# Counting edges for 16 nodes at a time instead of 32, with eight source parts instead of four

## The chip, the cores and the metric

The kernel runs on one core of one Trainium2 chip. The metric is the device time of one execution in microseconds (us); where several runs are given, their median counts. Lower is better.

## What is computed

One layer of a graph network on 1250 nodes with 768 features and 41250 edges (20000 random pairs in both directions and a loop for each node, sorted by target). Cut to what matters:

```
xn  = layernorm(x)
x   = x + gat(gat1(xn), edges) + random_feature_attention(xn) @ proj
x   = x + mixture_of_experts(layernorm(x))

gat:  e = leaky_relu(al_s[src] + al_d[dst]);  softmax of e over the edges of a target
      out = segment_sum(h[src] * alpha, dst)
mix:  phi = exp(x_head @ rf - |x_head|^2 / 2)
      out = phi_q @ (phi_k^T v) / (phi_q @ sum(phi_k))
```

The kernel does not walk the edges in the two attention layers. It first counts, for each target node and each source node, how many edges run between them, and then works with the dense 1250 x 1250 table of counts.

## The kernel before

The program goes through phases one after the other: a norm phase (`norm_phase`), two halves of the random feature attention (`mix_half_phase`, four heads each, followed by `numerator`), the projection, the two graph layers, and the experts. Each phase is a block with one instruction stream per engine; semaphores order the streams within it, and the block ends when all engines are through.

The table of counts is made in the mix halves, among the matrix products. `norm_phase` loads the edges, 128 to a row and 324 rows (`EROWS`), and turns them so that a row of edges lies along the 128 partitions. For each edge it makes a key, target times `SPLIT` plus the part of the source (`keyT`), and the source's place in its part of `SLO` nodes (`sloT`). A window is a group of `WIN` target nodes, so `WIN * SPLIT` is 128 keys, and there are `NW` windows. For each window `norm_phase` also works out which rows of edges can hold its targets (`spans`, lines 280 to 313): the start of the second step and the end, in steps of `RB` rows, two steps at least. An all-reduce over partitions on GpSimd stands in the middle of that.

In a mix half, VectorE makes for each row of edges two tables of zeros and ones, `CA` (128 edges by 128 keys, line 665, one operation for all rows of a step) and `CB` (128 edges by `SLO` places, line 671, one operation a row). TensorE multiplies them (line 807), and the sum over the rows of a window in one PSUM tile `S` is the table of counts for these targets, 128 by `SLO`. A short product (line 818) closes the sum, ScalarE copies it out of PSUM (line 729), and SyncE stores it in DRAM (line 636). The tables lie in a ring of `RING` steps. VectorE and TensorE both load the two numbers of a window's span into registers (lines 620 and 621), run the first step, and then loop over the others; a step's place in the ring is worked out in registers too, and so are the addresses of its rows. With `RB` 5, 40 windows and two steps each there are 400 rows.

The half itself goes over ten tiles of 125 nodes. For tile t TensorE turns q and k (`turn`, line 773), makes the q, k and v products of the next tile (`gemm`, line 762, twelve matmul records each), the features of k (`features`, line 781, in two parts of two heads) and keys times values (`keys_values`, line 790). The order is written out by hand, and so is the place of the two windows of a tile in it:

```
turn(0, t); gemm(0, t+1); window(2t); turn(1, t); gemm(1, t+1); features(t, 0)
window(2t+1); features(t, 1); gemm(2, t+1); keys_values(t)
```

The last tile of a half has no products of a next tile. ScalarE squares q and k for their norms (line 736), copies the turned q and k (lines 738 and 743), takes the exponential of the features (lines 747 and 750) and copies the counts, in a fixed order. VectorE evacuates q, k and v with their bias (lines 701 and 713), sums the squares (lines 706 and 707), makes the tables for the windows, and multiplies slices of the first graph weight with attention vectors (line 689).

Of the kernel before, what the change touches and what calls it, by code (L numbers as in the profile page):

```python
# [10 lines left out]
ALU = mybir.AluOpType  # L11
# [3 lines left out]
N = 1250  # L15
NT = 10
# [12 lines left out]
RB = 5  # L29
# [3 lines left out]
WIN = 32  # L33
NW = 40
SPLIT = 4
SLO = 314
# [102 lines left out]
def norm_phase(nc, cx, x, ident, xnT, src, dst, keyT, sloT, spans, counting, rf_dram, rfT, rf_loaded, load_next):  # L139
# [19 lines left out]
    DIV = (1 << DIV_SHIFT) // RB + 1  # L159
    assert FULL < EGP and EGP * EG == EROWS  # L160
    assert all(n * DIV >> DIV_SHIFT == n // RB for n in range(EROWS + RB))
    with ExitStack() as st:
# [63 lines left out]
        def _(dve):  # L226
# [4 lines left out]
            step(dve.tensor_scalar(hi[:], sf[:], float(SLO), None, ALU.is_ge))  # L231
            for part in range(2, SPLIT):
                step(dve.scalar_tensor_tensor(hi[:], sf[:], float(part * SLO), hi[:], ALU.is_ge, ALU.add))
# [339 lines left out]
def mix_half_phase(nc, cx, half, rfT, rf_loaded, xnT, ident, w, brow, w_loaded, b_loaded, attn, gnn_w1, a_src, a_dst,  # L573
# [6 lines left out]
    RING = 4  # L580
# [14 lines left out]
    with ExitStack() as st:  # L595
        qT = sb(nc, st, tag + "qT", [A, HH, N])
        kv = sb(nc, st, tag + "kv", [128, HH, 2, A])
        with ExitStack() as st1:
# [47 lines left out]
            def _(dve):  # L646
# [7 lines left out]
                with dve.register(tag + "count_turn_dve") as turn:  # L654
# [41 lines left out]
                    for t in range(NT):  # L696
# [12 lines left out]
                        window(PER * t)  # L709
                        dve.wait_ge(v_done, t + 1)  # L710
                        if t >= 1:
                            dve.wait_ge(kv_step, t)
# [3 lines left out]
                        window(PER * t + 1)  # L716
                        for n in range(t * columns // NT, (t + 1) * columns // NT):
                            attention_column(n)
                dve.wait_ge(kv_step, NT)
# [3 lines left out]
            @block.scalar  # L723
            def _(act):
                def keep_counts(i):
                    act.wait_ge(counted, i + 1)
                    if i >= 2:
                        act.wait_ge(s_stored[i % 2], 16 * (i // 2))
                    act.activation(cout[i % 2][:], S[:], ACT.Copy).then_inc(s_evac, 1)

                for t in range(NT):
                    for c, (evac, squared, ready) in enumerate(((q_evac, qsq, q_ready), (k_evac, ksq, k_ready))):
                        act.wait_ge(evac, t + 1)
                        if t >= 1:
                            act.wait_ge(ready, t)
                        act.activation(sq[:, c, :, :], qs[:, c, :, 0:MD], ACT.Square).then_inc(squared, 1)
                    act.wait_ge(q_turned, t + 1)
                    act.activation(qT[:, :, t * P:(t + 1) * P], TQ[:], ACT.Copy).then_inc(qT_done, 1)
                    keep_counts(PER * t)
                    act.wait_ge(k_turned, t + 1)  # L740
                    if t >= 1:
                        act.wait_ge(phi, 2 * t)
                    act.activation(kT[:], TQ[:], ACT.Copy).then_inc(kT_done, 1)
                    act.wait_ge(phi, 2 * t + 1)
                    if t >= 1:
                        act.wait_ge(kv_step, t)
                    act.activation(phik[:, 0:2, :], PH[:], ACT.Exp).then_inc(exped, 1)
                    keep_counts(PER * t + 1)
                    act.wait_ge(phi, 2 * t + 2)
                    act.activation(phik[:, 2:4, :], PH[:], ACT.Exp).then_inc(exped, 1)  # L750

            @block.tensor
            def _(pe):
# [31 lines left out]
                def keys_values(t, stop):  # L785
                    pe.wait_ge(exped, 2 * t + 2)
                    pe.wait_ge(v_evac, t + 1)
                    for h in range(HH):
                        for m in range(2):
                            last = pe.matmul(KV[h // 2][:, h % 2, m, :], phik[:, h, m * 128:(m + 1) * 128],  # L790
# [7 lines left out]
                with pe.register(tag + "count_turn_pe") as count:  # L798
# [25 lines left out]
                    for t in range(NT):  # L824
# [4 lines left out]
                        window(PER * t, *span(pe, half * PER * NT + PER * t))  # L829
                        turn(1, t)  # L830
                        if more:
                            gemm(1, t + 1, k_done, k_evac)
                        features(t, 0)
                        window(PER * t + 1, *span(pe, half * PER * NT + PER * t + 1))
                        features(t, 1)
                        if more:
                            gemm(2, t + 1, v_done, v_evac)
                        keys_values(t, not more)
# [1854 lines left out]
```

## Time and profile before

| | |
|---|---|
| median of 3 runs | 2090.27 us |
| lowest and highest | 2078.87 and 2092.76 us |
| the profiled execution's own time | 2086.34 us |
| its span, first to last instruction | 2084.6 us |
| mean granted TensorE clock | 0.977 |
| TensorE busy | 1991.5 us, 96% of the span |
| VectorE busy | 1168.3 us, 56% |
| ScalarE busy | 449.5 us, 22% |

The times of rows are microseconds from the start of the span. PE is TensorE's matmul, PEld its weight load, DVE VectorE, ACT ScalarE, POOL GpSimd, SP SyncE; a q behind an engine's name is its instruction queue with the register work, waits and branches, which doesn't count as busy. L807 is line 807 of the kernel. A matmul's end is modelled and reaches into the next one's time, so a block of matmuls lasts from its start to the next block's start.

### The profile page before, as it was taken

How to read it: one execution, taken by the hardware profiler on the slowest of the kernel's cores; microseconds unless marked ns; L12 is line 12 of the kernel's file. 1: busy time of each engine (PE TensorE's matmuls, PEld its weight loads, DVE VectorE, ACT ScalarE, POOL GpSimd, SP SyncE). 2: the span in 40 equal slices, each digit the busy share in tenths (PEclk: the TensorE clock that was granted, in tenths of full speed). 3: DMA queues.
4: the chain of work that ended last, by engine and by line, in shares of the span. 5: the costliest groups of instructions: out<-in, count | busy, mean ns of one | idle time of the engine just before them, and what ended most of it. 6: DMA issues, size and time to landing. Idle time of an engine off the chain costs nothing. (4 is left out here: it accounts for less than half of the span.)

```text
span 2084.6 us, 32353 instructions
## 1 busy us (share of the span) xinstructions
PE 1991.5 (96%) x9933; PEld 1469.9 (71%) x9934; DVE 1168.3 (56%) x2548; ACT 449.5 (22%) x822; POOL 176.6 (8%) x181
## 2 busy tenths in 40 slices
PE   4999899998989998999999999999997999999998
PEld 3666666666648887888888855556655777777776
DVE  6666436652565664888888652167764333333343
ACT  3222222222002321222222200004321222222222
POOL 0000000000000000000000000000001333222232
PEclk9999999998999999999999999999997999999999
DMA  7000220002645350743333244444225888899654
GB/s 257 22 17 20 93 107 17 20 17 74 217 120 171 121 155 32 221 146 102 122 101 112 82 153 156 151 134 142 90 74 196 271 249 241 252 284 289 180 136 83
DMA packets 81192, 282.79 MB, mean 136 GB/s; under 512 B 11689, under 2 KB 32225, under 8 KB 71490
## 3 DMA queue, kind: packets, MB, share of 16 engines
q1 hardware_dynamic: 59138, 211.02, 30.4%
q0 software_dynamic: 14848, 56.18, 11.1%
q10 hardware_dynamic: 7104, 14.26, 2.0%
q8 instruction: 59, 0.97, 0.2%
q14 instruction: 43, 0.35, 0.1%
HBM read 217.43 MB, written 63.99 MB: 135 GB/s over the span
## 5 line engine op out<-in xcount | busy, mean ns | idle before, releaser
L1379 PE MATMUL gat_Z<-h_head,first_rest 125*125 125x256 f32 (+1 forms) x1600 | 355.5, 381 | 3.3 <-DVEq L1283 3.3
L1379 PEld LDWEIGHTS gat_Z<-h_head,first_rest 125*125 125x125 f32 x1600 | 298.4, 189 | 49.2 <-issue 4.0
L762 PE MATMUL mix_G<-mix_w,xnT 128*125 128x384 f32 x720 | 243.0, 488 | 0.0
L762 PEld LDWEIGHTS mix_G<-mix_w,xnT 128*125 128x125 f32 x720 | 133.3, 189 | 85.1 <-issue 2.7
L2400 DVE TENSOR_SCALAR ex_idS<-ex_ids 128x1 int32 x52 | 8.0, 153 | 204.5 <-DMA out_rows<-ex_y,ex_idS 204.5
L2487 PE MATMUL ex_PH<-ex_xT,w_and_experts 128*128 128x128 f32 x936 | 111.1, 278 | 1.7 <-issue 0.2
L2487 PE MATMUL ex_PH<-ex_xT,ex_w 128*128 128x128 f32 x936 | 111.0, 278 | 0.8
L2487 PEld LDWEIGHTS ex_PH<-ex_xT,w_and_experts 128*128 128x128 f32 x936 | 106.5, 192 | 2.7 <-issue 2.7
L2497 PE MATMUL ex_PY<-w_and_experts,ex_hT 128*128 128x384 f32 x312 | 107.5, 495 | 0.3 <-ACT ex_hT L2434 0.3
L2497 PE MATMUL ex_PY<-ex_w,ex_hT 128*128 128x384 f32 x312 | 107.4, 494 | 0.3 <-ACT ex_hT L2434 0.3
L2487 PEld LDWEIGHTS ex_PH<-ex_xT,ex_w 128*128 128x128 f32 x936 | 106.5, 192 | 1.5 <-issue 1.3
L2370 DVE SCALAR_TENSOR_TENSOR ex_Q<-posm,offs,ex_iota 125x1280 bf16<-125x1280 f32 x54 | 83.8, 1551 | 38.4 <-issue 38.4
L2349 POOL DMA_INDIRECT out_rows<-ex_y,ex_idS x52 | 82.6, 1588 | 258.3 <-DVE ex_y L2402 202.2
L665 DVE SCALAR_TENSOR_TENSOR mix_count_A<-count_ikey,count_off,keyT 128x640 f32 x80 | 70.5, 881 | 41.0 <-issue 40.8
L671 DVE TENSOR_SCALAR mix_count_B<-count_islo,sloT 128x314 f16 x400 | 91.6, 298 | 0.0
L2442 ACT ACTIVATE ex_y<-ex_PY,ex_gate 128x384 f32<-128x384 f32 x52 | 30.2, 580 | 260.2 <-DMA out_rows<-ex_y,ex_idS 207.6
L2497 PEld LDWEIGHTS ex_PY<-w_and_experts,ex_hT 128*128 128x128 f32 x312 | 57.2, 190 | 38.2 <-ACT ex_hT L2434 0.7
L2497 PEld LDWEIGHTS ex_PY<-ex_w,ex_hT 128*128 128x128 f32 x312 | 57.3, 190 | 38.1 <-ACT ex_hT L2434 0.6
L499 PE MATMUL proj_Y<-mix_w,proj_aT 128*125 128x384 f32 x240 | 79.7, 490 | 0.0
L1004 DVE TENSOR_TENSOR h_head<-first_Y,h_head 125x256 f32<-125x256 f32 x80 | 33.9, 424 | 81.2 <-ACT h_head L1075 54.4
L2434 ACT ACTIVATE ex_hT<-ex_PH,ex_b1T 128x128 f32<-128x128 f32 x156 | 55.0, 367 | 107.2 <-PE ex_PH L2487 96.1
L1359 ACT ACTIVATE gat_oT<-gat_T 128x500 f32<-128x500 f32 x40 | 23.5, 587 | 249.1 <-PE gat_T L1389 249.1
(399 smaller groups left out, 3120.8 us busy)
## 6 DMA issues: line engine op xcount, KB each, us to landing
w_and_experts<-in_L_ffn_W SPq DMA_DIRECT2D x32, 1152.0 KB, 8.2
ex_w<-in_L_ffn_W SPq DMA_DIRECT2D x32, 1152.0 KB, 7.9
first_wide<-c_dram SPq DMA_DIRECT2D x40, 546.9 KB
h1T_dram<-gat_oT ACTq DMA_DIRECT2D x40, 250.0 KB, 2.0
mix_w<-in_L_mix_qkv_w SPq DMA_DIRECT2D x6, 1152.0 KB, 12.6
ct_dram<-mix_count_out SPq DMA_DIRECT2D x40, 157.0 KB, 2.1
mix_w_slice<-in_L_gnn_W SPq DMA_DIRECT2D x6, 1024.0 KB, 10.8
proj_w2s<-in_L_gnn_W SPq DMA_DIRECT2D x4, 1536.0 KB, 9.5
```

The source lines that it names most:

```text
L499: last = pe.matmul(Y[b][j][:], aT[b][:, k, :], w[:, k, j * 384:(j + 1) * 384], start=(k == 0), stop=(k == KD - 1))
L665: dve.scalar_tensor_tensor(CA[:, bass.ds(s * RB, RB), :], ikey[:].unsqueeze(1).to_broadcast([128, RB, 128]), off[:, win:win + 1], keyT[:, ...
L671: last = dve.tensor_scalar(CB[:, bass.ds(s * RB + b, 1), :], islo[:].unsqueeze(1), sloT[:, bass.ds(r + b, 1)], None, ALU.is_equal)
L762: last = pe.matmul(G[c][:], xnT[:, k, t * P:(t + 1) * P], w[:, k, c, :], start=(k == 0), stop=(k == KD - 1))
L1004: dve.tensor_tensor(C(n, i, j), bank[:, 0:HC], old, ALU.add).then_inc(add, 1)
L1379: last = pe.matmul(Z[b][j][:], wt[b][:, s, :], h[hd][0:P, s, j * HC:(j + 1) * HC + j], start=(s == 0), stop=(s == NT - 1))
L2349: pool.indirect_dma_start(out, bass.IndirectOffsetOnAxis(ap=idS[:, 0:1], axis=0), y[:], None, compute_op=ALU.add).then_inc(added, 16)
L2370: dve.scalar_tensor_tensor(Q[:], posm[:, :, bass.ds(e, 1)].to_broadcast([P, NT, SLOT]), 1.0 if first else offs[:, bass.ds(at, 1)], iot[:]. ...
L2434: act.activation(hT[:, m, :], PH[m][:], ACT.Gelu, bias=b1T[:, bass.ds(act.snap(e * KM + m), 1)]).then_inc(h_gelu, 1)
L2442: act.activation(y[:, 384:768], PY[1][:], ACT.Copy, scale=gate[:, slot]).then_inc(y_a, 1)
L2487: last = pe.matmul(PH[m][:], w1[b][:, k, m * 128:(m + 1) * 128], xT[:, k, :], start=(k == 0), stop=(k == KD - 1))
L2497: last = pe.matmul(PY[j][:], hT[:, k, :], w2[b][:, k, j * 384:(j + 1) * 384], start=(k == 0), stop=(k == KM - 1))
```

## The change

A window becomes 16 target nodes, and a source has eight parts of 157 nodes, so there are still 128 keys but 80 windows, and a row of `CB` and the tile `S` have 157 columns. A step has three rows, and the ring eight steps. Each tile of a half now has four windows instead of two. The last stands behind keys times values, which is issued in two parts of two heads with a wait each; the second features come after the v product. On ScalarE the squares of the next tile move from the start of a tile to the place between the third and the fourth copy of counts. The part of a source is worked out by a multiplication and a shift instead of comparisons.

```diff
-RB = 5
+RB = 3
-WIN = 32
-NW = 40
-SPLIT = 4
-SLO = 314
+WIN = 16
+NW = 80
+SPLIT = 8
+SLO = 157
...
-            step(dve.tensor_scalar(hi[:], sf[:], float(SLO), None, ALU.is_ge))
-            for part in range(2, SPLIT):
-                step(dve.scalar_tensor_tensor(hi[:], sf[:], float(part * SLO), hi[:], ALU.is_ge, ALU.add))
+            step(dve.tensor_scalar(si[:], sf[:], float(PART), None, ALU.mult))
+            step(dve.tensor_scalar(si[:], si[:], PART_SHIFT, None, ALU.logical_shift_right))
+            step(dve.tensor_copy(hi[:], si[:]))
...
-    RING = 4
+    RING = 8
...
                         window(PER * t)
+                        window(PER * t + 1)
                         dve.wait_ge(v_done, t + 1)
                         if t >= 1:
-                            dve.wait_ge(kv_step, t)
+                            dve.wait_ge(kv_step, 2 * t)
...
-                        window(PER * t + 1)
+                        window(PER * t + 2)
+                        window(PER * t + 3)
...
-                for t in range(NT):
+                def squares(t):
...
+                squares(0)
+                for t in range(NT):
                     act.wait_ge(q_turned, t + 1)
                     act.activation(qT[:, :, t * P:(t + 1) * P], TQ[:], ACT.Copy).then_inc(qT_done, 1)
                     keep_counts(PER * t)
...
-                    act.wait_ge(phi, 2 * t + 1)
-                    if t >= 1:
-                        act.wait_ge(kv_step, t)
-                    act.activation(phik[:, 0:2, :], PH[:], ACT.Exp).then_inc(exped, 1)
                     keep_counts(PER * t + 1)
-                    act.wait_ge(phi, 2 * t + 2)
-                    act.activation(phik[:, 2:4, :], PH[:], ACT.Exp).then_inc(exped, 1)
+                    for j in range(2):
+                        act.wait_ge(phi, 2 * t + j + 1)
+                        if t >= 1:
+                            act.wait_ge(kv_step, 2 * (t - 1) + j + 1)
+                        act.activation(phik[:, 2 * j:2 * j + 2, :], PH[:], ACT.Exp).then_inc(exped, 1)
+                    keep_counts(PER * t + 2)
+                    if t + 1 < NT:
+                        squares(t + 1)
+                    keep_counts(PER * t + 3)
...
-                def keys_values(t, stop):
-                    pe.wait_ge(exped, 2 * t + 2)
+                def keys_values(t, j, stop):
+                    pe.wait_ge(exped, 2 * t + j + 1)
                     pe.wait_ge(v_evac, t + 1)
-                    for h in range(HH):
+                    for h in range(2 * j, 2 * j + 2):
...
-                        window(PER * t, *span(pe, half * PER * NT + PER * t))
+                        at = half * PER * NT + PER * t
+                        window(PER * t, *span(pe, at))
                         turn(1, t)
                         if more:
                             gemm(1, t + 1, k_done, k_evac)
+                        window(PER * t + 1, *span(pe, at + 1))
                         features(t, 0)
-                        window(PER * t + 1, *span(pe, half * PER * NT + PER * t + 1))
-                        features(t, 1)
                         if more:
                             gemm(2, t + 1, v_done, v_evac)
-                        keys_values(t, not more)
+                        features(t, 1)
+                        window(PER * t + 2, *span(pe, at + 2))
+                        keys_values(t, 0, not more)
+                        keys_values(t, 1, not more)
+                        window(PER * t + 3, *span(pe, at + 3))
```

## Rows read from the trace of the kernel before

**Rows 1.** The page, first part: busy time of TensorE, share of the span, instructions.
```profile
PE 1991.5 (96%) x9933; PEld 1469.9 (71%) x9934; DVE 1168.3 (56%) x2548; ACT 449.5 (22%) x822; POOL 176.6 (8%) x181
```

**Rows 2.** Windows: stretch, us, busy PE, PEld, DVE, ACT, POOL, granted clock, DMA share, GB/s.
```profile
92.84:111.70 18.86, 18.86 (x93) 12.85 (x92) 11.92 (x37) 4.06 (x8) 0.00 (x0) 1.00 0.06 18
224.81:240.90 16.09, 11.28 (x56) 6.41 (x55) 9.81 (x31) 3.24 (x6) 0.00 (x0) 0.89 0.06 21
...
229.10:232.50 3.40, 2.00 (x10) 1.22 (x9) 3.40 (x13) 1.62 (x3) 0.00 (x0) 1.00 0.13 47
232.50:235.90 3.40, 3.24 (x12) 1.53 (x13) 1.47 (x6) 0.20 (x1) 0.00 (x0) 0.50 0.00 0
```

**Rows 3.** Timeline of TensorE in the middle tile: start, duration, engine, line, operation.
```profile
93.27 4.04 PE L762 MATMUL mix_G<-mix_w,xnT 128*125 128x384 f32 x12
97.14 1.51 PE L807 MATMUL mix_count_S<-mix_count_B,mix_count_A 128*128 x10
...
98.52 0.65 PE L773 MATMUL mix_TQ<-ident,mix_qs 125*97 125x125 f32 x4
...
106.06 4.04 PE L762 MATMUL mix_G<-mix_w,xnT 128*125 128x384 f32 x12
109.93 1.92 PE L790 MATMUL mix_KV<-mix_vs,mix_phik 125*128 125x97 f32 x16
```

**Rows 4.** TensorE's queue in the tile's first window: ns, first and last start.
```profile
L620 PEldq TENSOR_LOAD <-spans x1: 307/307/307, 92.6 to 92.6; - x1
...
L803 PEldq MOVE  x2: 37/37/37, 94.0 to 95.6; - x2
...
L816 PEldq COMPARE_BRANCH  x1: 76/76/76, 97.1 to 97.1; - x1
```

**Rows 5.** ScalarE's timeline, and TensorE's queue loading the next span, in two tiles.
```profile
99.20 0.59 ACT L743 ACTIVATE mix_kT<-mix_TQ 97x500 f32<-97x500 f32 x1
...
106.26 0.60 ACT L750 ACTIVATE mix_phik<-mix_PH 125x512 f32<-125x512 f32 x1 [0.51 <-PE mix_PH L781]
...
230.04 0.59 ACT L743 ACTIVATE mix_kT<-mix_TQ 97x500 f32<-97x500 f32 x1 [0.23 <-PE mix_TQ L773]
...
L620 PEldq TENSOR_LOAD <-spans x1: 562/562/562, 99.8 to 99.8; - x1
...
L620 PEldq TENSOR_LOAD <-spans x1: 445/445/445, 230.7 to 230.7; - x1
```

**Rows 6.** VectorE's queue, windows of the middle tile; and its attention columns.
```profile
L620 DVEq TENSOR_LOAD <-spans x1: 307/307/307, 94.4 to 94.4; - x1
...
L671 DVEq FUSED_REGOPS  x5: 82/93/93, 91.4 to 92.3; - x5
...
L677 DVEq COMPARE_BRANCH  x2: 43/43/43, 94.2 to 98.8; - x2
...
L689 DVE CUSTOM_DVE_ANT_0 mix_junk<-mix_w_slice,mix_a 128x512 f32<-128x512 f32 x24 | 15.4, 683 | 0.0
```

**Rows 7.** Timelines of the last tile of half 0, and the counts' copy and store.
```profile
227.92 1.28 PE L807 MATMUL mix_count_S<-mix_count_B,mix_count_A 128*128 x5 [0.47 <-DVE mix_count_B L671]
229.16 0.18 PE L818 MATMUL mix_count_S<-count_islo,count_zero 128*128 128x16 f16 x1
...
237.50 2.02 PE L790 MATMUL mix_KV<-mix_vs,mix_phik 125*128 125x97 f32 x16 [0.69 <-ACT mix_phik L750]
...
239.56 1.03 DVE L721 COPY mix_kv<-mix_KV 128x388 f32<-128x388 f32 x2 [5.60 <-PE mix_KV L790]
...
L729 ACT ACTIVATE mix_count_out<-mix_count_S x40: 432/432/434, 61.0 to 475.4; 128x314 f32<-128x314 f32 x40
...
DMA to landing us min/median/max: 1.9/2.1/2.4
```

**Rows 8.** Groups of the norm phase: busy us, mean ns of one, idle before.
```profile
L233 DVE SCALAR_TENSOR_TENSOR edge_hi<-edge_sf,edge_hi 108x384 f32<-108x384 f32 x2 | 1.1, 558 | 0.1
...
L304 DVE TENSOR_SCALAR edge_allb<-edge_allb 108x40 f32<-108x40 f32 x1 | 0.2, 184 | 0.0
```

More of the change, by code:

```diff
@@ L159, in norm_phase @@
     DIV = (1 << DIV_SHIFT) // RB + 1
+    PART_SHIFT = 17
+    PART = (1 << PART_SHIFT) // SLO + 1
+    assert all(n * PART >> PART_SHIFT == n // SLO for n in range(N)) and N * PART < 1 << 24
     assert FULL < EGP and EGP * EG == EROWS
@@ L715, in _ @@
                                           ).then_inc(v_evac, 1)
-                        window(PER * t + 1)
+                        window(PER * t + 2)
+                        window(PER * t + 3)
                         for n in range(t * columns // NT, (t + 1) * columns // NT):
                             attention_column(n)
-                dve.wait_ge(kv_step, NT)
+                dve.wait_ge(kv_step, 2 * NT)
                 for j in range(2):
@@ L783, in features @@
                     last.then_inc(phi, 1)
-                def keys_values(t, stop):
-                    pe.wait_ge(exped, 2 * t + 2)
+                def keys_values(t, j, stop):
+                    pe.wait_ge(exped, 2 * t + j + 1)
                     pe.wait_ge(v_evac, t + 1)
-                    for h in range(HH):
+                    for h in range(2 * j, 2 * j + 2):
                         for m in range(2):
-                            last = pe.matmul(KV[h // 2][:, h % 2, m, :], phik[:, h, m * 128:(m + 1) * 128],
+                            last = pe.matmul(KV[j][:, h % 2, m, :], phik[:, h, m * 128:(m + 1) * 128],
                                              vs[:, h, :], start=False, stop=stop, skip_group_check=True)
```

## Prediction

> **What bounds the kernel now.** I first read the page's first part: TensorE is busy 96% of the span, far ahead of any other engine [rows 1], so what counts is how the change alters TensorE's stream in the two mix halves, where all the counting is. Next come the windows of one tile: TensorE is busy 18.86 of 18.86 us at full clock [rows 2], and eighteen of the twenty tiles are alike, 18.85 us from one's first transposes to the next one's. The timeline of that tile shows the order: transposes, q product, count, transposes, k product, features, count, features, v product, keys times values, one block beginning where the last one lets go [rows 3]. A count window holds TensorE for 1.38 us (97.14 to 98.52), so counting takes 2.76 us of a tile.
>
> Then I looked at the instruction queue that feeds TensorE, because the matmuls of a count take their addresses from registers. For the first window of that tile the queue's rows run from the load of the span at 92.6 us to the loop's branch at 97.1 us [rows 4]: 1.3 us for two loads and their register work, 1.6 us for the first step of five rows, 1.5 us for the second, then the branch. That is 4.5 us of issuing for 1.38 us of matmuls. It costs nothing now because each window stands behind a product of 3.87 us (93.27 to 97.14), and the queue issues while the product runs. Where no product covers it, in the last tile of a half, the cost shows: five rows take 1.24 us there (227.92 to the closing product at 229.16) [rows 7], 0.248 us a row against 0.135 us in the covered tile, and TensorE is busy only 11.28 of 16.09 us [rows 2].
>
> How far ahead the queue may run decides the rest. Before the second window the queue has passed the features' matmuls, which wait for the copy of kT. That copy ends at 99.20 + 0.59 = 99.79 us and the load of the span starts at 99.8 us; in the last tile the copy ends at 230.63 us and the load starts at 230.7 us [rows 5]. I read this as: a matmul that waits holds back the register load behind it.
>
> **The change, part by part.** *TensorE's own work.* Counting the edges of the reference's list by target, 16 nodes touch at most six rows of 128 edges, so every one of the 80 windows takes two steps of three rows: 480 rows where there were 400. A row has 157 columns in place of 314. No row of before has that width; by columns it is 0.067 us (half of 0.135), and the nearest product with so few columns, keys times values, takes 1.77 us for 16, 0.11 us each (109.93 to 111.70) [rows 2, 3]. I take 0.07, nearer to the first since that product is f32 and these are bf16. A window is then 6 x 0.07 + 0.03 = 0.45 us, four are 1.8 us, and the engine alone would need 18.85 - 2.76 + 1.8 = 17.9 us a tile, 0.95 us less.
>
> *Issuing.* The loads, the loop and its branch are per window, so they double. A step of three rows loses two rows of 0.248 us: 1.1 and 1.0 us. A window costs 1.3 + 1.1 + 1.0 us, and 0.3 us for the branch and the closing product, which is an estimate: 3.7 us, four per tile 14.8 us, where two of before took 9.6 us. Each queue item between is cheap: from the branch at 97.1 to the load at 99.8 us twenty pairs of weight load and matmul went through, with the wait for kT in the same 2.7 us [rows 4, 5], so a pair costs between nothing and 0.13 us; I take 0.025.
>
> *Where the cover is.* Windows 0, 1 and 2 of a tile still stand behind the q, k and v products (transposes or features with it, 4.3 to 4.8 us). Window 2 may start issuing only when the first features have been through ScalarE's exponential, 0.8 us later, and still has 4.0 us for its 3.7. I cost these three at nothing; with loads 0.25 us longer (0.56 where the first took 0.31 us, rows 4 and 5) each cover is used up. Window 3 has none: it stands behind the two parts of keys times values, whose second part waits for the second exponential. Call e the end of the second features block. The exponential starts 0.2 us after it and takes 0.60 us (106.06, then 106.26) [rows 3, 5], so the second part is let through at e + 0.85; its eight pairs 0.2; loads 1.3; steps 2.1; branch and closing 0.3: window 3 ends at e + 4.75. The engine alone would be there at e + 0.45 + 1.77 + 0.45 = e + 2.67. **The stall is 2.1 us a tile**, so a tile takes 17.9 + 2.1 = 20.0 us, 1.15 us more than now. Behind it wait the next tile's transposes and q product, on the same queue, and nothing gives the time back. Eighteen tiles: 20.7 us.
>
> *The last tile of each half* has no products. Four windows at 3.7 us, 1.7 us between the first features and their exponential, and 0.8 us for the pushes make 17.3 us, against 14.7 us now (224.81 to the end of the last block, 237.50 + 2.02) [rows 2, 7]: 2.6 us each, 5.2 together.
>
> *The end of a half.* Now VectorE's copy of kv ends it, 1.1 us after TensorE (239.56 + 1.03 us). Afterwards window 3 comes last: ScalarE's copy (0.43 us for 314 columns, about 0.35 for 157), then SyncE's store, 2.1 us to landing, and SyncE waits for it at the block's end [rows 7]: 2.7 us. That adds 1.6 us, 3.2 for both halves. The other 78 stores land long before anyone reads them; cost nothing.
>
> *VectorE.* From its load at 94.4 us to its branch at 98.8 us a window takes its queue 4.4 us [rows 6]; four rows fewer at 0.22 us each make 3.5 us, 14.0 us for four. Attention columns (2.4 of 0.64 us, rows 6), evacuations and norms add some 4 us: 18 us, under 20.0. Ring of 8 steps: VectorE may be four windows ahead, and is not waited for. The squares move behind the third count on ScalarE; they start about e + 1.1 and the norms end about e + 3, before the next transposes ask for them at e + 4.75. Cost nothing; cover 1.7 us.
>
> *First phase.* The parts by multiply and shift replace two operations of 0.56 us by one of 0.36 more or less, hidden by the wait for x. Twenty operations on 40 columns get 80: up to 0.04 us each on 0.18 [rows 8], between nothing and 0.8 us, I take 0.7, since VectorE ends that phase.
>
> **Sum:** 20.7 + 5.2 + 3.2 + 0.7 = 30 us. The profiled execution took 2086.3 us (span 2084.6), so 2116; the median of the runs is 3.9 us above it, so **2120 us**.
>
> A sentence of the Trainium skill speaks against my reading of [rows 5]. Perfetto Trace Analysis, section Tensor Engine Instruction (MATMUL, LD_WEIGHTS), says that a matmul is pushed into a hardware wait queue, waits there for its semaphores, and that the sequencer is free for the next instruction at once. By that rule the load would not be held, and the change would cost what the second case below gives; the two rows of a load starting on the kT copy's end stand against it.
>
> **The rivals.** *The queue is not held by waiting matmuls.* Then window 3's loads are issued while features run, and only the evacuation of window 2 holds its rows: loads to e + 1.3, steps and close to e + 3.7, a stall of 1.0 us, a tile of 18.95 us. 18 x 0.1 + 5.2 + 3.2 + 0.7 = 11 us: 2101 us. For it: the queue runs ahead of running products freely. Against: [rows 5].
> *Not slower, the other side: issuing is covered everywhere.* If the queue issues window 3 during window 2's products, the price is -0.95 us x 20 = -19 us: 2071 us. It decides once a window's issue needs less than 1.8 us behind keys times values; the last tile's 0.248 us a row and the loads' 1.3 us speak against it.
> *The clock falls in each tile.* In the last tile the granted clock is 1.0 up to 232.5 us, after 3.40 us with TensorE busy 2.00, and 0.50 (1.2 GHz) to 235.9 us [rows 2]. The new tile has about 0.9 us empty and then rows of 0.07 at a pitch of 0.25 us before the transposes. Should such a stretch follow in each tile, half of 3.4 us is lost in eighteen: 31 us more, 2151 us. For it: the thinness of those rows; against: dense products follow at once.
> *VectorE becomes the bound*, if its window stays at 4.4 us (a shorter row that is no cheaper): 4 x 4.4 + 4 = 21.6 us a tile, 18 x 2.75 + 9 = 58 us: 2148 us. It decides above 4.0 us a window.
> That the change does not do what it says (third steps in some windows) is ruled out by the edge list, six rows at most.
>
> **How the numbers follow.** Forecast 0.60 (its own bounds: a row of 0.11 us instead of 0.07 adds 0.7 us a tile, longer loads 0.25, cheaper pushes take 0.2: 2114 to 2137 us); no holding 0.17; covered everywhere 0.04; clock 0.10; VectorE 0.09. A measurement here tells about 1%, 21 us, from no change. The range from the second case to the clock's, 2101 to 2151 us, leaves out the covered case and the fringes. Faster by over 1%: 0.03, part of the covered case and mishaps. Within 1%: 0.17 + 0.02 + 0.03 of the forecast's low end = 0.22. Slower: 0.75.
>
> **What would show it.** A tile of about 20.0 us from one transposing block to the next of its kind, with three counts of about 0.45 us and the fourth spread over 1.7 us at a pitch near 0.25 us, its first row about 0.9 us after keys times values; the load of window 3 starting right after the second exponential; a last tile near 17 us; SyncE's last store ending the half. I am wrong if the load of window 3 starts before that exponential ends, if the granted clock leaves 1.0 inside a half, if counts wait for VectorE, or if the first three windows also come late.

## The result, and the profile after

The changed kernel takes 2127.44 us (median of four runs, 2123.07 to 2132.16) against 2087.11 us before (2078.87 to 2092.76): a ratio of 1.0186, 95% interval 1.0162 to 1.021. That is some 39 us more by the ratio and 40.3 us between the medians. The forecast was 2120 us, its range 2101 to 2151. The profiled execution took 2130.04 us, its span is 2128.3 us.

The page's first part, which answers [rows 1]:

```profile
PE 2014.1 (95%) x10053; PEld 1480.6 (70%) x10054; DVE 1195.7 (56%) x2708; ACT 453.4 (21%) x862; POOL 182.1 (9%) x181
```

TensorE is busy 22.6 us longer though its counts got shorter. Where that comes from, the windows of five stretches show (columns as in [rows 2]): one tile, the beginnings of three others, and the last tile of the first half with what follows it.

```profile
77.35:80.76 3.41, 3.41 (x9) 2.17 (x9) 2.09 (x9) 0.79 (x2) 0.00 (x0) 0.50 0.08 24
98.66:118.62 19.96, 19.33 (x97) 12.99 (x98) 13.52 (x45) 4.30 (x10) 0.00 (x0) 1.00 0.06 18
138.79:142.20 3.41, 3.41 (x9) 2.01 (x8) 2.09 (x9) 0.68 (x2) 0.00 (x0) 0.50 0.08 24
...
200.23:203.64 3.41, 3.41 (x9) 2.17 (x9) 1.75 (x8) 0.85 (x2) 0.00 (x0) 0.50 0.08 24
...
244.60:268.49 23.89, 18.44 (x60) 11.75 (x60) 10.18 (x33) 4.34 (x10) 0.00 (x0) 0.50 0.23 68
```

A tile takes 19.96 us instead of 18.86. The granted clock, 1.00 through the same tiles before, now falls to 0.50 (1.2 GHz) for 3.41 us at the beginning of some tiles, and from the last tile of the half it stays there for 23.89 us.

TensorE's timeline of that tile (start, duration, engine, line, operation) answers [rows 3]; L818 is a row of a count, L829 the closing product.

```profile
99.23 4.04 PE L773 MATMUL mix_G<-mix_w,xnT 128*125 128x384 f32 x12
103.10 0.58 PE L818 MATMUL mix_count_S<-mix_count_B,mix_count_A 128*128 x6
103.52 0.17 PE L829 MATMUL mix_count_S<-count_islo,count_zero 128*128 128x16 f16 x1
103.55 0.65 PE L784 MATMUL mix_TQ<-ident,mix_qs 125*97 125x125 f32 x4
...
114.04 0.59 PE L818 MATMUL mix_count_S<-mix_count_B,mix_count_A 128*128 x6
114.46 0.17 PE L829 MATMUL mix_count_S<-count_islo,count_zero 128*128 128x16 f16 x1
114.49 2.00 PE L801 MATMUL mix_KV<-mix_vs,mix_phik 125*128 125x97 f32 x16
116.62 0.74 PE L818 MATMUL mix_count_S<-mix_count_B,mix_count_A 128*128 x3
117.72 0.75 PE L818 MATMUL mix_count_S<-mix_count_B,mix_count_A 128*128 x3 [0.35 <-issue]
118.49 0.18 PE L829 MATMUL mix_count_S<-count_islo,count_zero 128*128 128x16 f16 x1
118.62 0.64 PE L784 MATMUL mix_TQ<-ident,mix_qs 125*97 125x125 f32 x4
```

The first three windows hold TensorE for 0.45 us each (103.10 to 103.55). The fourth holds it from 116.62 to 118.62, 2.0 us for the same six rows, and "issue" stands between its steps. ScalarE's timeline gives the end of the second exponential, 114.24 + 0.60 = 114.84 us:

```profile
114.24 0.60 ACT L757 ACTIVATE mix_phik<-mix_PH 125x512 f32<-125x512 f32 x1 [4.14 <-PE mix_PH L792]
```

And TensorE's queue (duration min/median/max in ns, first and last start), as in [rows 4, 5]. In each row the first start, or for the branch the last, belongs to the fourth window:

```profile
L623 PEldq TENSOR_LOAD <-spans x2: 299/304/309, 114.9 to 118.7; - x2
...
L814 PEldq MOVE  x2: 37/37/37, 116.2 to 117.3; - x2
...
L827 PEldq COMPARE_BRANCH  x2: 76/76/76, 113.8 to 118.4; - x2
```

The load starts at 114.9 us, when the exponential lets the second part of keys times values go; the steps follow at 116.2 and 117.3, the branch at 118.4: 3.5 us of issuing, all after the wait. In the other 17 tiles that have products of a next tile the load comes as close behind that exponential, 0.07 to 0.09 us. The load of the next tile's first window, at 118.7, follows the branch.

Last, the end of the half, which answers [rows 7]: TensorE's timeline and ScalarE's, then the stores' line from 240 to 266 us.

```profile
255.70 3.70 PE L801 MATMUL mix_KV<-mix_vs,mix_phik 125*128 125x97 f32 x16
...
259.98 0.22 PE L829 MATMUL mix_count_S<-count_islo,count_zero 128*128 128x16 f16 x1
263.61 6.87 PE L400 MATMUL mix_F<-mix_qT,mix_rfT 97*128 x12 [3.41 <-ACTq L417]
...
260.26 0.30 ACT L734 ACTIVATE mix_count_out<-mix_count_S 128x157 f32<-128x157 f32 x1 [4.16 <-PE mix_count_S L829]
```

```profile
L639 SPq DMA_DIRECT2D ct_dram<-mix_count_out x5: 319/320/320, 242.0 to 260.6; - x5
...
DMA to landing us min/median/max: 1.7/1.9/2.1
```

The last store is issued at 260.6 us, when the copy of counts ends; the numerator's first product (L400) comes at 263.61.

From such starts in the two profiled executions, the 43.7 us between their spans split like this (KV: keys times values, first product of a tile; a half is taken to start with the product that sets its KV sums to zero; F: first product of the numerator):

| stretch | before, us | after, us | difference | in the forecast |
|---|---|---|---|---|
| start to the first half | 39.55 | 41.80 | +2.3 | +0.7 |
| to the first KV, two halves | 64.38 | 63.01 | -1.4 | +2.3 (two tiles) |
| 16 tiles, KV to KV | 301.65 | 325.51 | +23.9 | +18.4 |
| last tiles, KV to KV, then to F | 39.2 | 52.5 | +13.3 | +8.4 |
| numerator to the second half | 38.92 | 39.62 | +0.7 | 0 |
| F of the second half to the end | 1600.9 | 1605.9 | +5.0 | 0 |

In twelve of the 16 tiles KV to KV is 19.87 to 20.03 us; in four, where the clock falls, it is 21.55 to 21.71. Of the last line, 4.3 us arose in the experts' phase, which the change doesn't touch: there it took 517.4 us before and 521.7 after, and in the twelve profiled executions of this document, none of which changes it, 517.4 to 524.4.

### The profile page after: what moved, and what is told of

Same layout as the page of the kernel before. It is cut to its first block and busy times, and to the rows that moved or that the text cites. A ratio compares the mean times of both kernels' runs of the same rounds, so it can differ in the third digit from the quotient of the medians.

```text
span 2128.3 us, 34311 instructions
## 1 busy us (share of the span) xinstructions
PE 2014.1 (95%) x10053; PEld 1480.6 (70%) x10054; DVE 1195.7 (56%) x2708; ACT 453.4 (21%) x862; POOL 182.1 (9%) x181
## 3 DMA queue, kind: packets, MB, share of 16 engines
q8 instruction: 63, 1.03, 0.2%
## 5 line engine op out<-in xcount | busy, mean ns | idle before, releaser
L773 PE MATMUL mix_G<-mix_w,xnT 128*125 128x384 f32 x720 | 250.1, 499 | 0.0
L668 DVE SCALAR_TENSOR_TENSOR mix_count_A<-count_ikey,count_off,keyT 128x384 f32 x160 | 98.9, 618 | 107.8 <-issue 85.2
L674 DVE TENSOR_SCALAR mix_count_B<-count_islo,sloT 128x157 f16 x480 | 97.6, 258 | 0.3
L818 PE MATMUL mix_count_S<-mix_count_B,mix_count_A 128*128 x480 | 67.6, 238 | 17.0 <-issue 10.2
L818 PEld LDWEIGHTS mix_count_S<-mix_count_B,mix_count_A 128*128 x480 | 41.6, 99 | 53.6 <-issue 42.6
```

The source lines that it names most:

```text
L668: dve.scalar_tensor_tensor(CA[:, bass.ds(s * RB, RB), :], ikey[:].unsqueeze(1).to_broadcast([128, RB, 128]), off[:, win:win + 1], keyT[:, ...
L674: last = dve.tensor_scalar(CB[:, bass.ds(s * RB + b, 1), :], islo[:].unsqueeze(1), sloT[:, bass.ds(r + b, 1)], None, ALU.is_equal)
L773: last = pe.matmul(G[c][:], xnT[:, k, t * P:(t + 1) * P], w[:, k, c, :], start=(k == 0), stop=(k == KD - 1))
L818: last = pe.matmul(S[:], CA[:, bass.ds(s * RB + b, 1), :].rearrange("p o k -> p (o k)"), CB[:, bass.ds(s * RB + b, 1), :].rearrange("p o k ...
```

## The experiments

The theory: the fourth window's loads, rows and branch are issued only when the wait for the second exponential ends, nothing covers them, and the gap also lets the clock fall. The rivals: the queue runs on past waiting matmuls; VectorE is the bound; the new order of the products costs by itself. All edits are to the kernel after the change where nothing else is said. Tile means the mean of the 16 periods from KV to KV, last tiles the sum that the table above calls so. Each ratio is to runs of the kernel before from the same occasion, whose medians lie between 2086.77 and 2090.05 us.

| run | us | ratio to before, 95% interval | tile, us | last tiles, us |
|---|---|---|---|---|
| before | 2087.11 | | 18.85 | 39.2 |
| after | 2127.44 | 1.0186 (1.0162 to 1.021) | 20.35 | 52.5 |
| e1_hoist | 2102.65 | 1.0063 (1.0042 to 1.0083) | 18.89 | 51.4 |
| e2_order | 2136.36 | 1.0217 (1.0194 to 1.024) | 21.22 | 46.7 |
| e3_twice_fourth | 2179.29 (one run) | | 23.64 | 56.3 |
| e4_twice_first | 2132.84 (one run) | | 20.53 | 55.1 |
| e5_static_pe | 2096.47 | 1.0043 (1.0029 to 1.0057) | 18.88 | 47.8 |
| e6_static_pe_before | 2080.73 | 0.9965 (0.9949 to 0.9981) | 18.85 | 31.3 |
| e7_order_squares | 2091.09 | 1.0017 (1.0005 to 1.003) | 18.91 | 41.8 |
| e8_static_both | 2076.33 | 0.9943 (0.9927 to 0.9959) | 18.04 | 42.5 |
| e9_last_tile | 2067.17 | 0.9899 (0.9875 to 0.9924) | 18.04 | 36.7 |
| e10_static_dve | 2127.48 | 1.0198 (1.0169 to 1.0227) | 20.36 | 52.4 |

**e1_hoist.** The loads of the third and the fourth window move ahead, past the waits.

```
+                        third = span(pe, at + 2)
                         features(t, 1)
-                        window(PER * t + 2, *span(pe, at + 2))
+                        fourth = span(pe, at + 3)
+                        window(PER * t + 2, *third)
                         keys_values(t, 0, not more)
                         keys_values(t, 1, not more)
-                        window(PER * t + 3, *span(pe, at + 3))
+                        window(PER * t + 3, *fourth)
```

> The two span loads of the third window stand before the second pair of features, those of the fourth window before the third window; nothing else is touched. Theory (the matmul that waits for the second exponential holds TensorE's instruction queue, so the 3.5 us of the fourth window's loads, rows and branch start only when it is released): the 1.3 us of the two loads leave that stretch, the tile goes from 19.9 us to 18.6 to 18.8, 18 tiles give back 20 to 23 us, and most of the four clock falls (1.7 us each) go with the shorter gap: 2098 to 2108 us. The fourth window's register loads stand ahead of the waiting matmul in the queue and only its two rows and its branch behind it. Rival (the queue runs ahead past waiting matmuls, and the stall before the fourth window is the VectorE's or the ring's): where the loads stand makes no difference, tile 19.9, 2127 us. Second rival (the queue is short of issue time over the whole tile): the loads are paid elsewhere and the tile stays over 19.5.

2102.65 us: the theory's number; 24.8 us come back. TensorE's timeline, and the window of eight tiles:

```profile
109.31 0.58 PE L818 MATMUL mix_count_S<-mix_count_B,mix_count_A 128*128 x6
...
109.76 2.01 PE L801 MATMUL mix_KV<-mix_vs,mix_phik 125*128 125x97 f32 x16
111.60 1.00 PE L818 MATMUL mix_count_S<-mix_count_B,mix_count_A 128*128 x6
112.62 0.18 PE L829 MATMUL mix_count_S<-count_islo,count_zero 128*128 128x16 f16 x1
112.75 0.64 PE L784 MATMUL mix_TQ<-ident,mix_qs 125*97 125x125 f32 x4
```

```profile
72.00:230.00 158.00, 155.04 (x802) 105.91 (x799) 110.18 (x362) 37.73 (x86) 0.00 (x0) 1.00 0.07 19
```

The fourth window follows keys times values at once and holds TensorE for 1.15 us (111.60 to the next transposes at 112.75), still stretched by its rows' issue, instead of 2.0 after a gap; the clock stays at 1.00. What is left of the loss is almost all in the last tiles, 51.4 us against 39.2. The tile is 18.89 us, not the 18.04 that e8 will show: something else has come next.

**e3_twice_fourth and e4_twice_first.** The same pair of extra loads in two places.

```
+                        span(pe, at + 3)
                         window(PER * t + 3, *span(pe, at + 3))
```

is e3, and e4:

```
+                        span(pe, at)
                         window(PER * t, *span(pe, at))
```

> The fourth window's two span loads are issued twice, behind the waiting matmul; the second pair's values are used. Theory (issue behind the wait is on the path): 1.3 us more a tile, tile 21.2 us, 18 tiles 23 us and the two last tiles 1.3 each: 2150 to 2156 us, more if the clock falls in more tiles than four (1.7 us each, 30 at most). Rival (issue runs ahead of the wait, or is hidden by what follows): the tile stays 19.9, 2127 to 2130 us.

> The same two extra loads, but of the first window, whose place follows the first projection's products. Theory (there the queue runs ahead of TensorE, so issue is hidden until its lead is used up): 0 to 0.6 us a tile, 0 to 11 us, and the last tiles 1.3 each since nothing covers them: 2129 to 2141 us. Rival (the queue is the bound over the whole tile, wherever the loads stand): 1.3 us a tile as with the fourth window, 2150 to 2156 us.

e4 cost 5 us: its tiles without a fall are 20.15 to 20.45 us, 0.35 more, so the cover of the first window still hid some 0.9 of 1.3 us, and the queue isn't short over the whole tile. e3 cost 52 us, twice what issue alone gives. TensorE's timeline behind keys times values in e3, and three windows: the stretch of low clock in that tile, the first tile, and that tile as a whole:

```profile
115.04 2.00 PE L801 MATMUL mix_KV<-mix_vs,mix_phik 125*128 125x97 f32 x16
118.47 0.79 PE L818 MATMUL mix_count_S<-mix_count_B,mix_count_A 128*128 x3 [1.43 <-issue]
...
121.37 6.20 PE L773 MATMUL mix_G<-mix_w,xnT 128*125 128x384 f32 x12
```

```profile
118.95:125.78 6.83, 6.50 (x17) 3.77 (x17) 4.97 (x17) 0.89 (x2) 0.00 (x0) 0.50 0.05 14
...
71.06:92.04 20.98, 19.24 (x98) 12.90 (x97) 13.13 (x43) 4.10 (x11) 0.00 (x0) 1.00 0.06 18
...
115.04:138.80 23.76, 21.98 (x100) 14.40 (x98) 13.17 (x43) 4.30 (x11) 0.00 (x0) 0.86 0.05 15
```

The fourth window starts 3.43 us after keys times values began (118.47 against 115.04) where the change has 2.13: 1.30 more, the price of two loads. The first tile, at clock 1.00, is 20.98 us, 1.0 to 1.1 more than the changed kernel's tiles without a fall. Fourteen of the 16 tiles take 23.76 to 23.94 us at a mean clock of 0.86, and what they take above the first, 2.9 us, is the clock: 0.50 for 6.83 us behind the gap, a q product of 6.20 us instead of 4.04. The rival "the clock falls in each tile", a miss for the change, is what a longer gap brings about.

**e2_order and e7_order_squares.** The order alone, with the sizes of before; then with one move on ScalarE.

```
-RB = 3
+RB = 5
-WIN = 16
-NW = 80
-SPLIT = 8
-SLO = 157
+WIN = 32
+NW = 40
+SPLIT = 4
+SLO = 314
...
-    RING = 8
+    RING = 4
...
-                        window(PER * t + 2, *span(pe, at + 2))
                         keys_values(t, 0, not more)
                         keys_values(t, 1, not more)
-                        window(PER * t + 3, *span(pe, at + 3))
```

In e7 also, on ScalarE:

```
                         act.activation(phik[:, 2 * j:2 * j + 2, :], PH[:], ACT.Exp).then_inc(exped, 1)
-                    if t + 1 < NT:
-                        squares(t + 1)
+                        if j == 0 and t + 1 < NT:
+                            squares(t + 1)
```

> The order of the products alone: the kernel after the change with the sizes of before (32 nodes, four source parts, five rows a step, a ring of four, two windows a tile, in the places of the first two), but with the features, the third projection, the keys and values in two parts and the squares as the change orders them. Theory (the loss is the fourth window's issue behind the exponential's wait, and new order costs nothing by itself): tile 18.85 us as before the change or up to 0.3 less or more, 2082 to 2094 us; no window stands behind the last exponential. Rival (the order of the products itself, with the features after the third projection and the two parts of keys and values right behind them, is what stalls TensorE): tile above 19.5, over 2100 us.

> The order of the products alone once more (sizes of before), with one move on ScalarE: the squares of the next tile between the two exponentials, as before the change, and not behind the second. In the run of the order alone VectorE stood idle 6.7 us in each tile for these squares, and TensorE's first window waited for its rows. Theory (the order's price at five rows a step is the squares behind the second exponential, which now waits for features that stand behind the third projection): VectorE has its lead back, tile 18.85 to 19.1, 2085 to 2097 us. Rival (the order of the products on TensorE costs by itself): tile 20 or more, over 2115 us.

Here my theory fell: the order by itself cost 46 us (2136.36 against 2090.05 in the same runs). VectorE's timeline in e2 says why, and TensorE's beside it:

```profile
117.27 0.55 DVE L709 TENSOR_REDUCE mix_nrm<-mix_sq 125x4 f32<-125x384 f32 x1 [6.66 <-ACT mix_sq L739]
...
122.87 1.35 PE L814 MATMUL mix_count_S<-mix_count_B,mix_count_A 128*128 x5 [0.24 <-issue]
124.73 1.32 PE L814 MATMUL mix_count_S<-mix_count_B,mix_count_A 128*128 x5 [0.51 <-DVE mix_count_B L674]
```

VectorE stands idle 6.66 us for the squares, because ScalarE makes them behind the second exponential, and that waits for the second features, which now stand behind the v product. Before the change the squares came behind the second exponential too, but that one ended ahead of the v product (106.26 + 0.60 us; the next transposes come at 111.70):

```profile
106.76 0.93 ACT L736 ACTIVATE mix_sq<-mix_qs 125x384 f32<-125x384 f32 x2
```

So in e7 the squares stand in another place than before the change, but early again. In e2 VectorE starts the next tile's first window late, and TensorE spends 3.27 us on that window (122.87 to the next transposes at 126.14) where it took 1.38. e7 moves only the squares and is at 2091.09, tile 18.91. So the order on TensorE costs little, 4 us; the late squares cost some 42 us where steps have five rows (ratios 1.0217 and 1.0017).

**e5_static_pe and e6_static_pe_before.** TensorE's windows without registers, after and before the change (RB is 3 and 5).

```
...
-                        rows(True)
-                        with pe.Fori(second, end, RB) as _:
-                            rows(False)
+                        for n in range(2 * i, 2 * i + 2):
+                            pe.wait_ge(hot, n + 1)
+                            for b in range(RB):
+                                at = (n + 1) % RING * RB + b
+                                last = pe.matmul(S[:], CA[:, at, :], CB[:, at, :], start=n == 2 * i and b == 0,
+                                                 stop=False, skip_group_check=True)
+                            last.then_inc(used, 1)
```

> The kernel after the change with TensorE's windows written out: two steps each, addresses and waits constant, so that TensorE issues no register load, no register move and no branch. Left out: the loop over a window's further steps, of which this edge list needs none. In the run with the hoisted loads VectorE's own cycle, from one tile's norms to the next, is 19.1 us (norms end at 112.6, the four windows with 5.5 us of issue among them, the evictions, the squares' wait, norms again), and the tile there is 19.17. Theory (behind TensorE's issue, VectorE comes next): the tile goes from 19.9 to 19.1 or 19.2, 14 us in 18 tiles, the clock falls go, 7 us, and the last tile of each half loses its issue, 6 to 12 us each: 2080 to 2095 us. Rival (TensorE's issue is the only limit, VectorE has room): the tile falls to what the engine needs, 18.2, another 16 us less: 2063 to 2079 us. Rival (the stall is not of issue): 2120 us or more.

> The same edit on the kernel before the change (two steps of five rows a window, constant addresses and waits on TensorE; the loop over further steps is left out). Theory (before the change TensorE's tile is bound by the engine's own work, 18.86 us without idle time, and its issue is hidden): tile 18.85, nothing in the full tiles, only the last tile of each half loses the 3 to 5 us that issue takes there: 2077 to 2084 us. Rival (register issue costs TensorE in each tile): over 9 us less than that, under 2070.

e6 came out as the theory had it; e5 is 1.5 us above its range, with a tile below the 19.1 expected. Before the change the full tile does not move (18.85 us): its issue was hidden, and only the last tiles gain, 31.3 against 39.2 us. After it, TensorE issues nothing and the tile is still 18.88 on the mean (18.04 to 19.76), as in e1. TensorE's and VectorE's timelines in e5:

```profile
111.66 0.67 PE L784 MATMUL mix_TQ<-ident,mix_qs 125*97 125x125 f32 x4 [1.03 <-DVE mix_qs L710]
...
105.72 0.62 DVE L668 SCALAR_TENSOR_TENSOR mix_count_A<-count_ikey,count_off,keyT 128x384 f32 x1 [1.30 <-issue]
...
114.34 0.62 DVE L668 SCALAR_TENSOR_TENSOR mix_count_A<-count_ikey,count_off,keyT 128x384 f32 x1 [2.08 <-issue]
...
```

TensorE's transposes wait for VectorE's norms, and VectorE stands idle ahead of its own windows while its loads are issued: 37.4 us in 29 stalls between 40 and 220 us, against 1.1 us in which it waits for squares.

**e8_static_both and e10_static_dve.** VectorE's windows written out, with TensorE's (e8) and without (e10).

```
-                        second, end = span(dve, win)
...
-                        rows(dve.snap(second - RB, min_val=0, max_val=EROWS - 2 * RB))
-                        with dve.Fori(second, end, RB) as r:
-                            rows(r)
+                        second = dve.value_load(spans[0:1, win:win + 1], min_val=RB, max_val=EROWS - RB)
+                        starts = dve.snap(second - RB, min_val=0, max_val=EROWS - 2 * RB), second
+                        for j, r in enumerate(starts):
+                            n = 2 * i + j
+                            at = (n + 1) % RING * RB
+                            dve.wait_ge(used, n + 1)
...
```

> The kernel after the change with both TensorE's and VectorE's windows written out: VectorE loads one number a window, the row of the second step, and has no loop and no register for its turn. Left out, as above: further steps, which this edge list never needs. Theory (VectorE's cycle is the limit behind TensorE's issue): VectorE loses one of two loads a window (about 0.65 us of the 1.3 us for two) and the loop's branch and moves, over 2.6 us a tile, and its cycle falls from 19.1 to 16.5 or less; the tile is then what TensorE's own work takes, 18.1 to 18.3: 16 to 19 us less than with TensorE alone written out, 2062 to 2078 us, faster than both kernels. Rival (VectorE was not the limit there): the same as with TensorE alone, within 4 us.

> The kernel after the change with only VectorE's windows written out (one load a window, no loop; further steps left out); TensorE's windows with their loads, rows and branch as the change has them. Theory (TensorE's own issue of the fourth window behind the second exponential sets the tile of the changed kernel, VectorE comes only after it): the tile stays 19.9 and the clock falls stay few, 2121 to 2130 us. Rival (VectorE is the bound of the changed kernel): the tile falls by what it fell between the two runs with TensorE written out, 0.8 us, to 19.1: 2107 to 2115 us.

The pair tells the limits apart. VectorE's relief alone is worth nothing: 2127.48 us, tile 20.36, so VectorE is not the bound of the changed kernel. The same relief is worth 20 us once TensorE issues nothing: every tile of e8 is 18.04 us, and VectorE has time to spare, as its timeline in e8 shows:

```profile
108.26 0.56 DVE L704 TENSOR_REDUCE mix_nrm<-mix_sq 125x4 f32<-125x384 f32 x1 [4.34 <-ACT mix_sq L736]
```

The wait of 4.34 us is for squares again, and costs nothing here: TensorE's tile has no wait in it. 18.04 against the 18.85 of e6 is what the smaller windows give TensorE itself: 0.81 us a tile.

**e9_last_tile.** e8 with another order in the last tile of each half; on ScalarE the third copy of counts stands ahead of the second exponential there.

```
                         if more:
                             gemm(2, t + 1, v_done, v_evac)
+                        else:
+                            window(PER * t + 2)
                         features(t, 1)
-                        window(PER * t + 2)
+                        window(PER * t + 2 if more else PER * t + 3)
                         keys_values(t, 0, not more)
                         keys_values(t, 1, not more)
-                        window(PER * t + 3)
+                        if more:
+                            window(PER * t + 3)
```

> The kernel with both engines' windows written out (further steps left out, as there), and in the last tile of each half another order: the third window between the two pairs of features, the fourth before keys and values, and ScalarE copies the third window's counts ahead of the second exponential. The other nine tiles are untouched. With both written out the numerator's first product came 7.9 and 8.1 us after the last keys and values began, as far behind as before these were written out, although TensorE issues nothing there: the keys and values took 3.7 us, the fourth window's copy ended 233.65, and ScalarE was let into the numerator at 236.03, 2.4 us later, about what a store of counts takes to land. Theory (the end of a half waits for the last store of counts to land, and before the change it waited only for the copy of keys and values): the store lands under keys and values, the numerator begins 1.5 to 3 us earlier in each half, more if the clock holds in the last tile: 2066 to 2073 us. Rival (the numerator waits for the keys and values and the copies on VectorE): nothing is won, 2075 to 2078 us.

2067.17 us, 1.0% under the kernel before, with the last tiles at 36.7 us against 42.5. The end of the first half on TensorE, in e8 and then in e9:

```profile
228.78 3.71 PE L796 MATMUL mix_KV<-mix_vs,mix_phik 125*128 125x97 f32 x16
232.28 1.00 PE L814 MATMUL mix_count_S<-mix_count_B,mix_count_A 128*128 128x157 bf16 x6
233.07 0.22 PE L817 MATMUL mix_count_S<-count_islo,count_zero 128*128 128x16 f16 x1
236.66 3.83 PE L400 MATMUL mix_F<-mix_qT,mix_rfT 97*128 x5 [3.37 <-ACTq L417]
```

```profile
228.18 1.00 PE L815 MATMUL mix_count_S<-mix_count_B,mix_count_A 128*128 128x157 bf16 x6
228.97 0.22 PE L818 MATMUL mix_count_S<-count_islo,count_zero 128*128 128x16 f16 x1
229.05 3.71 PE L797 MATMUL mix_KV<-mix_vs,mix_phik 125*128 125x97 f32 x16
234.73 5.75 PE L400 MATMUL mix_F<-mix_qT,mix_rfT 97*128 x9 [1.97 <-ACTq L417]
```

With the store under keys times values the numerator begins 1.97 us after TensorE's last product instead of 3.37, and 5.68 us after the last keys times values began instead of 7.88 (4.62 instead of 8.08 in the second half). Of these 2.2 us, 1.4 are the shorter wait, the rest the fourth window's own work, which no longer stands between. In the second half the clock has a share: it is granted 1.00 from 464.75 to 468.16 us, where e8 has 0.50 to 478.13. The last tiles account for 5.8 us, and the two profiled executions differ by 5.5; what else is in the 9 us between the medians no trace shows. This version, like e5, e6, e8 and e10, holds only for an edge list whose windows all need two steps; e1 keeps the loop.

## Why the prediction was right

The main mechanism was right, and the sum was low: the loss was forecast at 30 us and is 40.3 between the medians, 43.7 between the profiled executions. Of the 14 us by which the profiled executions exceed the sum, 5.7 lie in stretches that the change doesn't touch. In the others it came out 12 us low, and 3.7 us too high in the first tiles, so part of the closeness is luck. The range of 50 us would also have held a queue that nothing holds (2101) and a fall of the clock in every tile (2151), so it is the rows and the experiments, not the number, that decide. Two of the prediction's own signs of being wrong did appear: the granted clock left 1.00 inside the halves, and counts waited for VectorE, 2.4 us in all, though only in the last tiles.

**The stall behind the second exponential** was the main term, and the mechanism is shown: the load starts at the exponential's end (114.9 against 114.84 us), the fourth window is done 4.58 us after the second features (114.04 to 118.62; 4.75 forecast), a tile without a fall is 19.87 to 20.03 us (20.0), moving 1.3 us of loads out of it gives 24.8 us back (e1), adding 1.3 there costs a tile 1.0 to 1.1 before the clock takes its share (e3), and adding them elsewhere a third of that (e4). The rival that the queue is not held would have had the load start under the features; it starts at the wait's end in the changed kernel too.
By the sentence of the Trainium skill, Perfetto Trace Analysis, section Tensor Engine Instruction (MATMUL, LD_WEIGHTS), the queue would be free again as soon as the waiting matmul is pushed. These starts do not agree with it.

Two rivals remain that the rows can settle: a separate wait in the queue, and a queue that is simply full. The queue's separate waits ahead of the two parts (line 798, for v) are over at 114.1 us. In e2 the transposes wait for VectorE's first norms, and in 18 tiles the first window's load starts 0.06 to 0.26 us after these are ready (in the tile below 118.2 after 117.86 + 0.17 us, with 15 matmuls still to start ahead of it; in the changed kernel's tile there are 12). The first row is the changed kernel's, the others are e2's:

```profile
L798 PEldq EVENT_SEMAPHORE  x2: 51/51/51, 114.0 to 114.1; - x2
...
117.86 0.17 DVE L710 TENSOR_SCALAR mix_qs<-mix_nrm 125x4 f32<-125x4 f32 x1
...
L623 PEldq TENSOR_LOAD <-spans x1: 297/297/297, 118.2 to 118.2; - x1
```

So the load follows the end of the wait, whichever engine ends it, and not a fixed place in the queue. By what means a waiting product holds the queue stays open.

**TensorE's own gain** was sized well: a window of 0.45 us, as measured, and a tile of 17.9 against the 18.04 of e8. The cover of the first three windows held.

**Two terms were mis-sized.** The last tiles and the ends of the halves cost 13.3 us, not 5.2 + 3.2 = 8.4: the sum priced their products at full clock, but the clock stood at 0.50 there for 23.89 us, and keys times values took 3.70 instead of about 1.9 us; the first half's last tile lasted 18.6 us (241.58 to 260.20), 17.3 forecast. In the second half, where the clock stood at 0.50 from 474.83 us before the change too, the difference is 5.6 us, in the first 7.7. That the last store of counts ends the half is shown by e9. And the clock fell in four of the 16 tiles, 1.7 us each, 6.7 us in all; the forecast had that only as a rival, for every tile or none. Against this stand the first tiles, 1.4 us shorter where 2.3 longer were forecast; why stays open.

**VectorE** was costed at 18 us a tile, under the 20.0 that TensorE needs. e10 shows that it does not bind, but its cycle is nearer 19: with TensorE's issue gone the tile stops at 18.88. "The squares cost nothing, cover 1.7 us" came true in the changed kernel: the norms end at 116.72 + 0.17 = 116.89 and the transposes come at 118.62 us.

```profile
116.72 0.17 DVE L710 TENSOR_SCALAR mix_qs<-mix_nrm 125x4 f32<-125x4 f32 x1
```

But that cover is the stall's own: without it the transposes wait for the norms (1.03 us in e5), there because of VectorE's loads and not of the squares. With five rows a step the late squares cost some 42 us (e2 against e7), a price that the prediction didn't look for. So the new order with the old sizes is as slow as the whole change, and cheap with the squares made early.

**The first phase**: VectorE's span operations on 80 columns took 0.77 us more, 0.7 forecast; the other 1.5 us ahead of the first half came from a wait for x, and between the twelve profiled executions the first KV varies from 70.9 to 73.7 us. The 4.3 us of the experts' phase lie within what that phase varies by.

## What to carry to other kernels

Work whose addresses come from registers costs issue time as well as engine time (here 3.5 us of issue for 0.45 us of matmuls), so price both. Put each such piece behind a product that is long enough to hide its issue, with no wait for another engine in between, and its loads ahead of any wait that is left. When such a stall is taken away, look for what it was hiding: here a second engine's loads, 0.84 us a tile. Small outputs that are stored at the end of a phase belong ahead of its last products where, as here, the phase waits for their landing.

## What was not expected of the hardware

The same thin stretch stood behind keys times values in all 16 tiles of the changed kernel, and the granted clock fell to 0.50 behind four of them, for 3.41 us; with 1.3 us more without work (e3) it fell in 15 of 16, in 14 of them for 6.83 us. In the first half of the changed kernel the falls begin at 77.35, 138.79 and 200.23 us, 61.44 us apart, in every third tile. The Trainium skill, TensorE: Matmul & The Clock Gate, section What's actually happening, says that the activity watch runs free of the program; these rows agree with it.

On VectorE two loads and their register work ahead of a window left the engine idle for 1.30 and 2.08 us (e5), against some 2.2 us for the window's own operations (105.72 us to its end near 107.9).
